# Half of the softmax sums from ScalarE in two attentions, a later time-bias step, and four destination columns in the last expert layer of a decoder

## The chip, the cores and the metric

The kernel runs on one core of a Trainium2 chip. The metric is the device time of one launch, in microseconds. One execution is also recorded by the hardware profiler, and all rows in this document come from such recordings.

## The reference, cut to what matters

The reference is a decoder of four layers on `x` of 16 x 128 tokens with 256 features. Each layer is `x = x + attention(layernorm(x))`, then a second mixing step with a context `ctx`, then a feed-forward step. Three of its twelve steps are touched.

```python
# layer 3, cross attention with a time bias ("l3x"): 16 heads of 16, 4 heads of values
pairwise_delta = |cumulative time of query - cumulative time of key|
scores = scores + time_bias_weight * log1p(pairwise_delta)
scores = scores + (1 - mask) * -1e9
w = softmax(scores);  out = (w @ v) @ Wo

# layer 2, feed-forward step, first half ("l2fa"): plain self attention, 16 heads of 16
w = softmax(q @ k.T * 0.25);  out = (w @ v) @ wo

# layer 3, feed-forward step ("l3f"): 8 experts, the best 2 of them for each token
out = zeros
for e in range(8):
    h = relu(xf @ W1[e] + b1[e]);  y = h @ W2[e] + b2[e]
    out = out + gate[:, e:e+1] * y
```

## The kernel before, in words

Every step of the decoder is a block. In a block each engine (TensorE, VectorE, ScalarE, GpSimd, and SyncE for transfers) has a program of its own in fixed order, and engines meet at semaphores. A block ends at a barrier.

**`attention_block`** serves six attentions. Its loop runs over `t` from 0 to `T + VALUES + 1`; in `l2fa` and `l3x` `T` is 32: 16 sequences (`NB`) times two sets of `HEADS = 8` heads, each set in two banks of `UNIT = 4` heads. At step `t`:

- TensorE makes the scores of `t` (L658), a slice of the projections of the next pair of sequences (L599 to L617: transposed rows, keys, queries, values), the transposition of the probabilities of `t - 3` (`turn`, L676), the product with the values of `t - 4` (L690, L695), and every second step the output projection (L631). There are three score banks, so the scores of `t + 1` wait until ScalarE has finished the exponentials of the first bank of `t`.
- VectorE adds the bias (L872, `l3x` only) and takes the maxima (L874), sums the exponentials of `t - 1` over the keys (L882) and inverts the sums (L888), empties projections (L785 in `l2fa`: the keys, which in `l3x` are ScalarE's), and copies the first bank of transposed probabilities (L898).
- ScalarE computes the exponentials, one instruction for each head (L1025, four to a bank), copies the second bank of transposed probabilities (L1041), empties some projections (L988: eight pieces of the keys in `l3x`, once for every four steps) and copies the output of the values (L1049), which the output projection L631 waits for.
- GpSimd multiplies the exponentials with the inverted sums (L953).

**The opening of `l3x`.** SyncE issues loads in this order: context, the times `fside` as `deltas`, the mask as `keywide` (spread over 128 partitions, 1 MB), context. TensorE's first instruction is L587, the running sums of the times, which waits for `deltas` and `keywide`. Then come the first query projection (from rows the block before left ready), the context's transposition, keys and values; then the four `bias_turns` (L627). VectorE copies the running sums (L842), spreads `deltas` into `dwide` in four instructions (L844), takes part in the projections and the layer norm's statistics, subtracts (L824), waits for ScalarE's absolute values and logarithms (L1014, L1016), and makes all four quarters of the bias (L861) before the first scores are touched.

**`sorted_experts_block`**, as `l3f`, sorts tokens by expert into tiles of 128 rows. There are always `NT = 39` tiles, some of them without real rows. SyncE loads the rows of tile `n` (L1259), TensorE transposes them (`turn`, L1398), multiplies by the first weights (`first_layer`, L1410) and the second (`second_layer`, L1420). As this is the last block, the results go straight into `out`: GpSimd fetches the rows so far (L1852), VectorE adds the tile's gated result (L1720), and GpSimd scatters the rows back (L1856). A token has two experts, so the fetch of a tile waits until the scatter of the tile before has landed. The rows that both transfers go to are computed by VectorE in `aim(n)` (L1684 to L1699, `dest`); there were two columns of `dest`, taken in turn.

VectorE's order in that loop is:

```python
for n in range(NT):
    if n + 1 < NT:
        relu(n + 1)
        aim(n + 1)
    if n + 2 < NT:
        empty_rows(n + 2)
    empty_out(n)
```

`aim(n)` waits for the scatter of tile `n - 2`. `empty_rows(n + 2)` (L1675) lets TensorE start the first weights of tile `n + 2`; `empty_out(n)` is L1715 and L1720. SyncE loads tile `n` after tile `n - 2` was transposed and aimed (`turned`, `dest_ready`).

## Time and profile before

| what | value |
|---|---|
| time, median of 3 runs | 2975.32 us (2972.42 to 2977.95) |
| the profiled execution's own time | 2969.33 us |
| its span in the profile | 2967.4 us |
| mean granted TensorE clock, share of full speed | 0.933 |
| `l2fa`, first to last scores | 1774.5 to 1923.1 us |
| `l3x`, first load to first scores | 2312.5 to 2336.0 us |
| `l0x`, first load | 243.8 us |
| `l3x`, first to last scores | 2336.0 to 2524.9 us |
| `l3f`, first fetch to last scatter | 2649.3 to 2956.5 us |

A row of the timeline has the start in us from the span's start, the length in us, the engine, the line and operation, what it writes and reads, how many instructions are merged, and in brackets how long the engine sat idle before it and what ended that. TensorE's multiplications are PE, its weight loads PEld, VectorE is DVE, ScalarE ACT, GpSimd POOL; a q behind the name is an engine's instruction queue. The ends of the multiplications are modelled, so a busy PE is not a full one.

### The profile page before, as it was taken

What the parts mean: (1) busy time and instruction counts of PE and PEld (TensorE: products, weight loads), DVE (VectorE), ACT (ScalarE), POOL (GpSimd) and SP (SyncE); (2) the same over time, 40 slices, a digit from 0 to 9 for tenths busy, and PEclk for the clock granted to TensorE, in tenths of its full rate; (3) what the DMA queues carried; (4) which work ended last, traced back from release to release, by engine and by line L of the source; (5) the groups of instructions that cost most, each with busy time, mean ns of one, the idle gap of its engine ahead of it and who ended that gap; (6) DMA issues with size and microseconds to landing.
All of it is one profiled execution on the core that took longest, in us unless ns stands there. A gap on an engine that the chain in (4) does not pass through costs nothing. (4 is left out here: it accounts for less than half of the span.)

```text
span 2967.4 us, 47859 instructions
## 1 busy us (share of the span) xinstructions
PE 2559.4 (86%) x16117; PEld 1874.6 (63%) x16117; DVE 1810.5 (61%) x4091; ACT 1313.7 (44%) x3205; POOL 808.7 (27%) x627
## 2 busy tenths in 40 slices
PE   4998989999688785999998989959969687869997
PEld 2666756666455453777676767649945465448886
DVE  7866976589788544344455559953355688444443
ACT  2334654266778234434343436623332565323332
POOL 5533520054000332222221216621110243132222
PEclk8999999999888798999999999979989898989999
DMA  9001000000200423000001010051120300531110
GB/s 321 2 1 49 14 19 1 15 1 1 65 4 1 109 87 125 29 1 1 1 1 50 12 42 31 2 206 37 37 76 1 90 12 1 182 118 49 51 49 26
DMA packets 152050, 142.43 MB, mean 48 GB/s; under 512 B 59948, under 2 KB 136770, under 8 KB 151428
## 3 DMA queue, kind: packets, MB, share of 16 engines
q1 hardware_dynamic: 139668, 110.61, 12.6%
q0 software_dynamic: 10560, 27.19, 2.7%
q8 instruction: 135, 2.21, 0.3%
q10 hardware_dynamic: 1584, 1.57, 0.2%
q14 instruction: 103, 0.84, 0.1%
HBM read 98.14 MB, written 43.02 MB: 48 GB/s over the span
## 5 line engine op out<-in xcount | busy, mean ns | idle before, releaser
L953 POOL TENSOR_TENSOR room<-room 128x1024 f32<-128x1024 f32 x144 | 273.1, 1896 | 464.0 <-DVE room L888 463.7
L882 DVE TENSOR_REDUCE room<-room 128x8 f32<-128x1024 f32 x144 | 174.1, 1209 | 0.0
L1420 PE MATMUL l3f_out<-room,Y 128*128 x624 | 141.0, 379 | 0.0
L953 POOL TENSOR_TENSOR room<-room,Y 128x1024 f32<-128x1024 f32 x32 | 60.7, 1896 | 252.0 <-DVE Y L888 252.0
L1420 PEld LDWEIGHTS l3f_out<-room,Y 128*128 128x128 f32 x624 | 115.6, 190 | 14.2
L1025 ACT ACTIVATE room<-l2a_scores,Y 128x128 f32<-128x128 f32 x256 | 71.9, 380 | 86.7 <-DVE Y L874 86.7
L609 PE MATMUL l2a_proj<-room 128*128 128x256 f32 x384 | 97.5, 398 | 11.6 <-ACT room L977 11.6
L2461 POOL DMA_INDIRECT sorted_rows<-room,l1f_place_i x32 | 31.0, 968 | 267.1 <-DVE l1f_place_i L2172 257.7
L1025 ACT ACTIVATE room<-l3x_scores,room 128x128 f32<-128x128 f32 x256 | 73.3, 401 | 55.3 <-DVE room L874 55.3
L1025 ACT ACTIVATE room<-l1a_scores,room 128x128 f32<-128x128 f32 x256 | 71.4, 386 | 58.6 <-DVE room L874 58.6
L1025 ACT ACTIVATE room<-l0x_scores,room 128x128 f32<-128x128 f32 x256 | 70.5, 384 | 59.4 <-DVE room L874 59.4
L1025 ACT ACTIVATE room<-l2fa_scores,room 128x128 f32<-128x128 f32 x256 | 71.4, 389 | 49.2 <-DVE room L874 49.1
L609 PEld LDWEIGHTS l2a_proj<-room 128*128 128x128 f32 x384 | 71.8, 196 | 24.7 <-issue 14.9
L1420 PE MATMUL l2fm_out<-room,Y 128*128 x368 | 83.1, 379 | 0.0
L914 POOL MEMSET room<- 128x3072 f32 (+1 forms) x4 | 9.4, 2338 | 269.1 <-POOLq L135 269.1
L1811 ACT COPY l3f_yn<-room 128x2048 f32 x39 | 74.5, 1911 | 16.4 <-DMA sorted_rows<-l3f_yn,l3f_place_i 16.2
L1410 PEld LDWEIGHTS l3f_hidden<-Y,l3f_yn 128*128 128x128 f32 x640 | 74.9, 195 | 10.7 <-DVE Y L1675 10.5
L1410 PE MATMUL l3f_hidden<-Y,l3f_yn 128*128 128x128 f32 x640 | 77.9, 281 | 4.3 <-DVE Y L1675 4.1
L1410 PE MATMUL l3f_hiddenT<-Y,l3f_yn 128*128 128x128 f32 x608 | 72.6, 278 | 7.2 <-DVE Y L1675 6.9
L1410 PEld LDWEIGHTS l3f_hiddenT<-Y,l3f_yn 128*128 128x128 f32 x608 | 69.5, 192 | 13.5 <-DVE Y L1675 13.4
L1856 POOL DMA_INDIRECT out<-Y,l3f_dest x39 | 39.1, 1002 | 135.2 <-DVE Y L1720 131.8
L3517 DVE TENSOR_TENSOR room<-room 128x2048 f32<-128x2048 f32 x32 | 72.2, 2289 | 3.9 <-ACT room L3623 2.6
(838 smaller groups left out, 6909.3 us busy)
## 6 DMA issues: line engine op xcount, KB each, us to landing
sorted_rows<-head SPq DMA_DIRECT2D x1, 16640.0 KB, 57.0
room<-in_L_ffn_w SPq DMA_DIRECT2D x16, 1024.0 KB, 13.0
room<-in_L_ffn_W SPq DMA_DIRECT2D x16, 1024.0 KB, 12.0
Y<-sorted_rows SPq DMA_DIRECT2D x62, 130.0 KB, 2.1
room<-in_ctx SPq DMA_DIRECT2D x24, 256.0 KB, 2.9
room<-sorted_rows SPq DMA_DIRECT2D x39, 130.0 KB, 2.1
room<-results SPq DMA_DIRECT2D x8, 512.0 KB, 7.1
room<-in_L_ffn_routed_w SPq DMA_DIRECT2D x4, 512.0 KB
```

Of the source, the lines that this page charges most:

```text
L609: mm = pe.matmul(bank[:, (c - i) * PT:(c - i + 1) * PT], w.v[kind][:, kc, c * P:(c + 1) * P], (y_of(g) if kind == "q" else c_of(g))[:, kc, ...
L882: dve.tensor_reduce(rsum[:, u % 2, :], p[:, u % (TURN + 1), :, :], AX.X, ALU.add)
L914: pool.memset(v[:, :, :, :], 0.0).then_inc(v_zeroed, 1)
L953: pool.tensor_tensor(p[:, u % (TURN + 1), :, :], p[:, u % (TURN + 1), :, :], rinv[:, u % (TURN + 1), :].unsqueeze(2).to_broadcast([P, HEAD ...
L1025: op = act.activation(p[:, t % (TURN + 1), a * UNIT + i, :], bank[:, i * P:(i + 1) * P], ACT.Exp, bias=nmx[:, t % 2, a * UNIT + i:a * UNIT ...
L1410: mm = pe.matmul(hidden[n % 2][a][:, q * P:(q + 1) * P], stage[:, n % 2, kc * F + f * P:kc * F + (f + 1) * P], rowsT[:, n % 2, kc, :], sta ...
L1420: mm = pe.matmul(obank[n % 2][:, 0:D], hT[:, n % 2, f, :], chip.room[:, bass.ds(at + (SLOT // 2 + f * D), D)], start=(f == 0), stop=(f == ...
L1811: act.copy(stage[:, n % 2, :], chip.room[:, bass.ds(at, KC * F)]).then_inc(staged, 1)
L1856: pool.indirect_dma_start(final_rows, bass.IndirectOffsetOnAxis(dest[:, n % 2:n % 2 + 1], 0), result[:, n % 2, :], None, bounds_check=TOK ...
L2461: pool.indirect_dma_start(table[:, :], bass.IndirectOffsetOnAxis(place_i[c][:, b:b + 1], 0), yn[:, b, :], None).then_inc(scattered, 16)
L3517: dve.tensor_tensor(hat[:, n % 2, those, :], hat[:, n % 2, those, :], aw[:, g % 2, j, those].unsqueeze(2).to_broadcast([P, HALF, NR]), ALU ...
```

## The change

It has three parts.

1. In `l3x` and `l2fa` the exponentials of heads 4 to 7 write their own sums (`accum_out`), and L882 sums only heads 0 to 3.
2. In the opening of `l3x` the matmul of the running sums goes behind the opening projections, on VectorE the spreading of `deltas` goes behind the emptied projections, and only the first quarter of the bias is made ahead of the loop, the others at steps 1 to 3.
3. In the last expert block `dest` has four columns, and `aim(n)` waits for the scatter of tile `n - 4` in place of `n - 2`.

```diff
+    SUMMED = UNIT if t_ in ("l3x", "l2fa") else HEADS
...
                 w.wait(pe)
-                if plan.mask == "timebias":
-                    pe.wait_ge(raw_loaded[0], 32)
-                    pe.matmul(out[:, 0:NB], chip.upper[:, :], deltas[:, :], start=True, stop=True).then_inc(ct_ready, 1)
...
-                for f in opening + bias_turns:
+                for f in opening:
+                    project((0, f))
+                if plan.mask == "timebias":
+                    pe.wait_ge(raw_loaded[0], 32)
+                    pe.matmul(out[:, 0:NB], chip.upper[:, :], deltas[:, :], start=True, stop=True).then_inc(ct_ready, 1)
+                for f in bias_turns:
                     project((0, f))
...
-                if plan.mask == "timebias":
-                    dve.wait_ge(ct_ready, 1)
-                    dve.tensor_copy(ctcol[:, :], out[:, 0:NB])
-                    for n in range(NB // 4):
-                        dve.tensor_copy(dwide[:, n * 4:n * 4 + 4, :], ...).then_inc(wide_ready, 1)
-                    dve.drain()
...
                 for f in opening:
                     if not by_scalar(f):
                         empty((0, f))
+                if plan.mask == "timebias":
+                    dve.wait_ge(raw_loaded[0], 32)
+                    for n in range(NB // 4):
+                        dve.tensor_copy(dwide[:, n * 4:n * 4 + 4, :], ...).then_inc(wide_ready, 1)
+                    dve.wait_ge(ct_ready, 1)
+                    dve.tensor_copy(ctcol[:, :], out[:, 0:NB])
+                    dve.drain()
                 if chip.has_head:
                     statistics()
...
+                def biased(n):
+                    dve.wait_ge(log_ready, n + 1)
+                    dve.scalar_tensor_tensor(out=bias[:, n * 4:n * 4 + 4, :], ...)
+                    dve.drain()
...
-                    for n in range(NB // 4):
-                        dve.wait_ge(log_ready, n + 1)
-                        dve.scalar_tensor_tensor(out=bias[:, n * 4:n * 4 + 4, :], ...)
-                    dve.drain()
+                    biased(0)
...
-                        dve.tensor_reduce(rsum[:, u % 2, :], p[:, u % (TURN + 1), :, :], AX.X, ALU.add)
+                        dve.tensor_reduce(rsum[:, u % 2, 0:SUMMED], p[:, u % (TURN + 1), 0:SUMMED, :], AX.X, ALU.add)
...
+                    if plan.mask == "timebias" and 1 <= t < NB // 4:
+                        biased(t)
...
-                        op = act.activation(p[:, t % (TURN + 1), a * UNIT + i, :], bank[:, i * P:(i + 1) * P], ACT.Exp, bias=nmx[...])
+                        h = a * UNIT + i
+                        if h < SUMMED:
+                            op = act.activation(p[:, t % (TURN + 1), h, :], bank[:, i * P:(i + 1) * P], ACT.Exp, bias=nmx[...])
+                        else:
+                            op = act.activation(p[:, t % (TURN + 1), h, :], bank[:, i * P:(i + 1) * P], ACT.Exp, bias=nmx[...],
+                                                accum_out=rsum[:, t % 2, h:h + 1])
...
+    DESTS = 4 if last else 2
...
-                    if n >= 2:
+                    if last and n >= 4:
+                        dve.wait_ge(returned[par], (n // 2 - 1) * 16)
+                    if not last and n >= 2:
                         dve.wait_ge(returned[par], n // 2 * 16)
...
-                    dve.scalar_tensor_tensor(out=dest[:, par:par + 1], ...).then_inc(dest_ready, 1)
+                    dve.scalar_tensor_tensor(out=dest[:, n % DESTS:n % DESTS + 1], ...).then_inc(dest_ready, 1)
```

The fetch and the scatter of GpSimd take their column with `n % DESTS` too.

## Rows read from the trace of the kernel before

**Rows 1.** Stretches: length, busy time (instructions) by engine, granted clock, DMA share, GB/s.

```profile
255.00:413.00 158.00, 153.60 (x1272) 107.68 (x1273) 139.12 (x267) 99.23 (x332) 77.88 (x50) 0.99 0.05 13
...
1774.50:1923.10 148.60, 136.59 (x1184) 103.31 (x1183) 136.91 (x266) 97.36 (x332) 94.42 (x66) 0.97 0.09 29
...
2336.00:2525.00 189.00, 149.66 (x1212) 111.25 (x1211) 156.95 (x288) 122.47 (x386) 67.03 (x40) 0.89 0.04 12
...
2660.00:2930.00 270.00, 258.88 (x1742) 234.81 (x1741) 113.03 (x448) 100.48 (x172) 69.72 (x69) 1.00 0.16 49
```

**Rows 2.** Timeline of the opening of l3x.

```profile
2319.74 0.58 PE L587 MATMUL l3x_out<-room,upper 128*128 128x16 f32 x2 [9.41 <-DMA room<-in_mask_BxS_ff]
...
2320.15 3.47 PE L609 MATMUL l3x_proj<-head,room 128*128 128x256 f32 x8
...
2330.04 4.55 PE L627 MATMUL l3x_proj<-upper,room 128*128 128x128 f32 x24 [2.28 <-ACT room L988]
...
2337.60 2.81 DVE L861 SCALAR_TENSOR_TENSOR room<-room,vecs 128x512 f32<-128x512 f32 x4 [0.21 <-issue]
...
2342.01 1.14 ACT L1025 ACTIVATE room<-l3x_scores,room 128x128 f32<-128x128 f32 x4 [1.07 <-DVE room L874]
```

**Rows 3.** Timeline of the opening of l0x, a block with the same order of projections.

```profile
246.58 0.82 PEld L604 LDWEIGHTS l0x_proj<-ident,room 128*128 128x128 f32 x4 [0.35 <-DMA room<-in_ctx]
```

**Rows 4.** Groups of VectorE's and ScalarE's instructions in l2fa: busy time, mean ns | idle before.

```profile
L874 DVE TENSOR_REDUCE room<-l2fa_scores 128x4 f32<-128x512 f32 x64 | 40.7, 678 | 4.7 <-PE l2fa_scores L658 4.6
L882 DVE TENSOR_REDUCE room<-room 128x8 f32<-128x1024 f32 x32 | 38.7, 1209 | 0.0
...
L1025 ACT ACTIVATE room<-l2fa_scores,room 128x128 f32<-128x128 f32 x256 | 71.4, 389 | 49.2 <-DVE room L874 49.1
```

**Rows 5.** Waits of TensorE in l2fa, 1776 to 1923 us: total, times, longest.

```profile
PE l2fa_probsT L676 <- DVE room L898: 5.4, 8, 0.8
```

**Rows 6.** Timeline of ScalarE in an earlier block that sums while it activates.

```profile
1171.03 0.19 ACT L2441 ACTIVATION_READ_ACCUMULATOR room<-X 128x1 f32 x1
1171.12 0.40 ACT L2441 ACTIVATE room<-X 128x256 f32<-128x256 f32 x1
```

**Rows 7.** Timeline of l3x around the emptied keys, two groups of four steps.

```profile
2396.19 1.10 PE L631 MATMUL l3x_proj<-room 128*128 128x256 f32 x4 [1.71 <-ACT room L1049]
...
2467.30 3.06 ACT L988 ACTIVATE room<-l3x_proj,block_of 128x256 f32<-128x256 f32 x8
...
2470.67 2.05 PE L631 MATMUL l3x_proj<-room 128*128 128x256 f32 x4 [1.71 <-ACT room L1049]
...
2472.51 3.62 PE L609 MATMUL l3x_proj<-room 128*128 128x256 f32 x8
```

**Rows 8.** Timeline of l3f, from one fetch to the next.

```profile
2791.93 0.16 DVE L1684 TENSOR_TENSOR vecs<-Y,vecs 128x1 f32<-128x1 f32 x1 [1.79 <-DMA out<-Y,l3f_dest]
...
2792.82 1.03 POOL L1852 DMA_INDIRECT Y<-out,l3f_dest  x1 [2.34 <-DMA out<-Y,l3f_dest]
...
2793.89 15.31 SPq L1259 DMA_DIRECT2D Y<-sorted_rows  x3
...
2795.57 0.48 DVE L1720 SCALAR_TENSOR_TENSOR Y<-Y,vecs 128x256 f32<-128x256 f32 x1 [1.44 <-DMA Y<-out,l3f_dest]
...
2796.39 1.13 DVE L1707 TENSOR_SCALAR Y<-l3f_hiddenT,vecs 128x128 f32<-128x128 f32 x4 [0.34 <-issue]
...
2800.10 1.03 POOL L1852 DMA_INDIRECT Y<-out,l3f_dest  x1 [2.25 <-DMA out<-Y,l3f_dest]
```

**Rows 9.** The chain that ended last, in order of time: two fetches of tiles without real rows.

```profile
2932.52 3.13 DMA Y<-out,l3f_dest
...
2940.01 2.15 DMA Y<-out,l3f_dest
```

**Rows 10.** DMA issues in l3f: count, median us from issue to landing.

```profile
Y<-out,l3f_dest POOLq DMA_INDIRECT x39, 2.9
out<-Y,l3f_dest POOLq DMA_INDIRECT x39, 2.5
```

More of the change, by code:

```diff
@@ L856, in _ @@
                     empty((0, f))
+                def biased(n):
+                    dve.wait_ge(log_ready, n + 1)
+                    dve.scalar_tensor_tensor(out=bias[:, n * 4:n * 4 + 4, :], in0=gap[:, n * 4:n * 4 + 4, :], scalar=w.v["tb"],
+                                             in1=keywide[:, n * TG:(n + 1) * TG].rearrange("p (j k) -> p j k", j=4), op0=ALU.mult, op1=ALU.add)
+                    dve.drain()
                 if plan.mask == "timebias":
                     dve.wait_ge(key_ready, 1)
-                    for n in range(NB // 4):
-                        dve.wait_ge(log_ready, n + 1)
-                        dve.scalar_tensor_tensor(out=bias[:, n * 4:n * 4 + 4, :], in0=gap[:, n * 4:n * 4 + 4, :], scalar=w.v["tb"],
-                                                 in1=keywide[:, n * TG:(n + 1) * TG].rearrange("p (j k) -> p j k", j=4), op0=ALU.mult, op1=ALU.add)
-                    dve.drain()
+                    biased(0)
                 for t in range(T + VALUES + 2):
@@ L1024, in exps @@
                     for i in range(UNIT):
-                        op = act.activation(p[:, t % (TURN + 1), a * UNIT + i, :], bank[:, i * P:(i + 1) * P], ACT.Exp, bias=nmx[:, t % 2, a * UNIT + i:a * UNIT + i + 1])
+                        h = a * UNIT + i
+                        if h < SUMMED:
+                            op = act.activation(p[:, t % (TURN + 1), h, :], bank[:, i * P:(i + 1) * P], ACT.Exp, bias=nmx[:, t % 2, h:h + 1])
+                        else:
+                            op = act.activation(p[:, t % (TURN + 1), h, :], bank[:, i * P:(i + 1) * P], ACT.Exp, bias=nmx[:, t % 2, h:h + 1],
+                                                accum_out=rsum[:, t % 2, h:h + 1])
                     op.then_inc(exps_done, 1)
@@ L1191, in sorted_experts_block @@
         row_at = chip.iota_i[:, 0:NT]
-        dest_f, dest = own("dest_f", [P, 2, 2]), own("dest", [P, 2], mybir.dt.uint32)
+        dest_f, dest = own("dest_f", [P, 2, 2]), own("dest", [P, DESTS], mybir.dt.uint32)
         hT = flat_y[:, 0:2 * F].rearrange("p (a f t) -> p a f t", a=2, f=HC)
@@ L1698, in aim @@
                     dve.drain()
-                    dve.scalar_tensor_tensor(out=dest[:, par:par + 1], in0=dest_f[:, par, 1:2], scalar=real[:, n:n + 1], in1=dump[:, n:n + 1], op0=ALU.mult, op1=ALU.add).then_inc(dest_ready, 1)
+                    dve.scalar_tensor_tensor(out=dest[:, n % DESTS:n % DESTS + 1], in0=dest_f[:, par, 1:2], scalar=real[:, n:n + 1], in1=dump[:, n:n + 1], op0=ALU.mult, op1=ALU.add).then_inc(dest_ready, 1)
                 def relu(n):
@@ L1851, in _ @@
                             pool.wait_ge(returned[(n - 1) % 2], ((n - 1) // 2 + 1) * 16)
-                        pool.indirect_dma_start(so_far, None, final_rows, bass.IndirectOffsetOnAxis(dest[:, n % 2:n % 2 + 1], 0),
+                        pool.indirect_dma_start(so_far, None, final_rows, bass.IndirectOffsetOnAxis(dest[:, n % DESTS:n % DESTS + 1], 0),
                                                 bounds_check=TOK - 1, oob_is_err=False).then_inc(fetched, 16)
@@ L1855, in _ @@
                     if last:
-                        pool.indirect_dma_start(final_rows, bass.IndirectOffsetOnAxis(dest[:, n % 2:n % 2 + 1], 0), result[:, n % 2, :], None,
+                        pool.indirect_dma_start(final_rows, bass.IndirectOffsetOnAxis(dest[:, n % DESTS:n % DESTS + 1], 0), result[:, n % 2, :], None,
                                                 bounds_check=TOK - 1, oob_is_err=False).then_inc(returned[n % 2], 16)
```

2 lines of the change are left out of this document (1 added, 1 removed).

## The prediction, made before the changed kernel ran

> **What bounds the kernel now.** I read the page first for the shares of the engines, then the stretches of the three touched blocks, then in each block the waits, the timeline and, for the last one, the chain that ended last. The blocks have different limits, so each edit is priced in its own.
>
> In the loop of `l2fa` TensorE is busy 136.6 of 148.6 us and VectorE 136.9 [rows 1]. The reader is to see that TensorE is nearly full: it idles 12.0 us, and in `l0x`, a loop of the same form, 4.4 of 158. So at most some 8 us are to be had there, however much VectorE is relieved. Its waits name VectorE's copy L898 with 5.4 us in 8 waits [rows 5].
>
> In the loop of `l3x` TensorE is busy 149.7 of 189 us at a granted clock of 0.89, VectorE 157.0 [rows 1]. Here no engine is full; the timeline shows a cycle of four steps. VectorE runs without a pause through two or three steps; then ScalarE empties the keys in 3.06 us, so its copy L1049 comes late, and TensorE waits 1.71 us with the output projection L631 [rows 7]. In the later group that L631 takes 2.05 us where the earlier one took 1.10: the clock fell from 2.4 to 1.2 GHz after TensorE had idled, and the projection behind it takes 3.62 us [rows 7].
>
> In the opening of `l3x` TensorE stands until 2319.74 for the mask's broadcast, 7.3 us after the block's first load at 2312.5 (table above) and after 9.41 us of standing idle [rows 2], though the query projection behind it needs no load of this block.
>
> In `l3f` GpSimd waits for VectorE's L1720 or for a landed scatter, and L1720 waits for the fetch [rows 8]: fetch, add, scatter, fetch is one serial chain. From 2660 to 2930 us TensorE ran 1742 matmuls at full clock [rows 1], 50 to a tile (32, 16 and 2 transposes), so 34.8 tiles: 7.75 us for a tile, of which TensorE is busy 7.43. The chain sets the pace, and TensorE is close behind.
>
> **The opening of `l3x`.** The query projection now starts with the block, about 2312.5 in place of 2320.15: 7.65 us earlier [rows 2]. It takes 3.47 us, to 2316.0. In `l0x` the context was there 2.8 us after its load (load at 243.8 in the table, transposition at 246.58 when it had landed [rows 3]), so here by 2315.3, no wait. Context, keys and values keep their distances and end near 2320, just behind the broadcast at 2319.7. The moved matmul L587 costs TensorE 0.58 us [rows 2] between the values and L627, where TensorE waited 2.28 us for the emptied keys [rows 2]; that wait covers it. Without that cover it would cost its 0.58. VectorE's spreading of the times is covered by the same wait. So L627 and all that follows on it comes 7.65 us earlier.
>
> The bias: four quarters took 2.81 us, 0.70 each [rows 2]. Now one stands before the first scores. ScalarE waited 1.07 us for VectorE at its first exponentials [rows 2], and only that much is gained, because behind it stand ScalarE's own logarithms and table load. The three other quarters go into steps 1 to 3: 2.1 us more on VectorE, against 3 x 0.53 us that it is relieved of (below), so 0.5 net; another 0.4 for ScalarE's longer steps there. Sum: -7.65 - 1.07 + 0.9 = -7.8; I take -8, bounds -5 (context late or broadcast still in the way) and -9.
>
> **The sums.** L882 takes 1209 ns for 1024 elements in a partition; L874, a reduction of 512, takes 678 [rows 4]. The halved L882 saves 0.53 us a step, 32 times in each block. ScalarE's price: before, four exponentials stood in 1.14 us [rows 2]; one lasts 0.39 [rows 4], so they follow each other by (1.14 - 0.39) / 3 = 0.25. With a sum a read of 0.19 us is added, and the next instruction starts 0.09 us after the read did, so a pair lasts as long as the activation itself (0.40 for 256 elements) [rows 6]. Here that is 0.39 in place of 0.25: 0.14 x 4, or 0.5 us a step (0.56 rounded down, as the mean of 0.39 holds stalled ones). No row shows an exponential of 128 elements with a sum; the bounds are 4 x 0.09 = 0.4 and 4 x 0.19 = 0.8 us.
>
> A rule beside it: the Trainium skill (ScalarE: Activation LUTs, What ACT_TABLE_LOAD costs) gives 280 ns + 0.833 ns for each element with a pointer as bias, and 93 ns of overlap between neighbours. By it an exponential takes 387 ns and follows by 294, so the sum would add only 0.09 to each, 0.37 us a step; the trace's 0.25 disagrees, and I go by the trace.
>
> *In `l2fa`* ScalarE is busy 97 of 149 us [rows 1], which hides 0.5 us a step. VectorE's L898 comes 0.53 us earlier in each of the 8 waits of 0.68 us: 8 x 0.53 = 4.3 us, and with a second halved sum in the same group a little more. -5.5, bounds 0 (TensorE takes no advantage) and -8 (the idle share of `l0x`).
>
> *In `l3x`* the cycle of four steps goes: two steps on VectorE (-0.53 each), then ScalarE's second four exponentials (+0.5), copy, keys, L1049, then TensorE to the next scores. Net -0.56, seven times: -4. What is queued behind the longer exponentials is L1041, L988 and L1049, and TensorE waits for the last. TensorE's own idle time ahead of L631 grows by 0.5 us, as it arrives 1.06 us earlier and is released 0.56 earlier. The clock fell in 4 of 6 groups although the wait was 1.71 us in both rows [rows 7], so the fall is not decided by that wait alone, and more idle time makes it likelier. At half clock L631 and L609 take 2.05 + 3.62 = 5.7 us, at full about half plus latencies, 3.0 (1.10 for L631): 2.7 us a fall. One more fall, taken at +2 for its chance. -2, bounds -14 (no fall any more: -4 and 4 x 2.7 back) and +5 (three more falls).
>
> **Four destination columns.** `aim(n + 1)` waited for a landed scatter, which ended at 2791.93 [rows 8]. But the fetch waits for that same landing, and VectorE then waits 1.44 us for the fetch anyway [rows 8]. TensorE gains `empty_rows` earlier, but L1720 waits for the fetch and not for TensorE. So the wait that goes is covered by the chain of transfers, and its removal alone is worth nothing. What is moved is the load of rows by SyncE, which follows `aim`. Before, it was issued at 2793.89, 1.07 us behind the fetch and 1.96 us behind the landing [rows 8]. After, `aim` follows `relu` at once: 2796.39 + 1.13 + 1.96 = 2799.5, which is 0.6 us ahead of the fetch at 2800.10 [rows 8]. Both fetches of [rows 9] carry no rows: 3.13 us beside a load, 2.15 without one. A full fetch takes 2.9 us where a full scatter, which has no load beside it, takes 2.5 [rows 10]. So the load costs a fetch about 0.4 us now. Ahead of the fetch its data may be through sooner: I take 0.1 us off, 34 full tiles: -3. Bounds: -0.32 x 34 = -11, where TensorE's 7.43 us a tile sets the pace, and +0.98 x 34 = +33, the full price of [rows 9] on top of today's.
>
> A rule speaks against this part: the Trainium skill (DMA: Bandwidth & Descriptors, Queues, rings and completion order) says a transfer's completion is written only after every earlier write of the same DMA engine, across queues. The page would make a load moved ahead delay each fetch's completion; the 3.13 against 2.15 us of the empty fetches agrees that a completion can wait for a load's data. By it the sum would end near the slow rival below.
>
> **The sum.** -8 - 5.5 - 2 - 3 = -18.5 us. It is made in the profiled execution, whose own time is 2969.33 us (span 2967.4 and 1.9 around it): 2950.8 there. The median of the runs is 6.0 us above that execution, so the forecast is 2975.3 - 18.5 = 2956.8 us. For this kernel 0.2%, 6 us, is about what a measurement can tell from no change.
>
> **The rivals.**
>
> *The last block speeds up to TensorE's pace.* The load leaves the fetch's way altogether. For it: 0.4 us a fetch to win. Against: load and fetch still start within 0.6 us of each other. -8 - 5.5 - 2 - 11 = -26.5: 2949 us.
>
> *The sums change nothing, only the opening gains.* In `l2fa` TensorE is full, in `l3x` ScalarE's 0.5 us or the clock eats VectorE's 0.53. For it: TensorE's 92% in `l2fa` [rows 1]. Against: the 5.4 us that TensorE waits for L898 [rows 5]. With the last block unchanged: -8, 2967 us. Should the broadcast still hold the opening (its bound, -5), the whole change is within what can be measured.
>
> *Slower: the row load stands in front of the fetch.* Place: the fetch L1852 in 34 tiles of `l3f`. Price: up to 0.98 us each. It eats the other 15.5 us of gain from 0.46 us a tile on and makes the kernel slower by over 0.2% from 0.63 on; at 0.98 it gives 2975.3 - 15.5 + 33 = 2993 us. For it: [rows 9]. Against: the load now starts earlier, and most of its data may be through before the fetch has its descriptors, whose making takes 1.03 us [rows 8].
>
> **How the numbers follow.** Forecast 0.55, with a range of its own of 2950 to 2963; last block at TensorE's pace 0.15; opening alone 0.18; load in front 0.12. The first two are faster, of the third 0.13; of the load's cases 0.05 end within 0.2% and 0.07 above. Faster 0.83, same 0.10, slower 0.07. The range, 2943 to 2972, takes in the first three with their bounds and leaves out the last.
>
> **What would show each step.** The first exponentials of `l3x` start about 21 us behind the block's first load, not 29.5. L882 on 512 elements near 0.68 us; reads of 0.19 us behind half of the exponentials, and four with sums in about 1.6 us. TensorE's wait for L898 in `l2fa` near 1 us. In `l3x` L631 still waiting for L1049, and longer than 1.71 us. In `l3f` no wait ahead of L1684, loads issued ahead of the fetches, and the fetch's median to landing against 2.9 us, which decides the last block. The prediction fails if that median rises by half a microsecond, or if TensorE's clock in `l3x` moves far from 0.89.

## The result, and the profile after

The changed kernel takes 2948.0 us (median of 4 runs, 2941.3 to 2950.5) where the kernel before takes 2973.9 (median of 4, 2972.4 to 2978.0). The medians lie 25.9 us apart; the ratio estimated from these runs is 0.989, with a 95% interval of 0.987 to 0.991, and a second comparison below gives 0.9888. So 26 to 33 us were gained where 18.5 were forecast. The time lies 2 us below the forecast's own range of 2950 to 2963 us and inside the wide one. The direction holds and each of the three parts gains, but the sizes are off, the last block's most.

The profiled execution has a span of 2946.8 us, 20.6 below the one before. The blocks ahead of `l2fa`, which the change doesn't touch, take up to 19 us more or less from one execution to another (`l2fa` opens at 1764.2 us before, at 1772.3 after, and between 1770 and 1784 in the other kernels below). So I compare blocks, not whole spans.

Three stretches, one in each touched block: length, busy time by engine, granted clock, DMA share, GB/s. They answer to [rows 1].

```profile
1783.00:1930.00 147.00, 138.72 (x1212) 104.49 (x1210) 125.37 (x273) 110.87 (x469) 96.41 (x67) 0.97 0.08 30
2337.00:2515.00 178.00, 147.29 (x1199) 109.02 (x1199) 136.62 (x277) 127.90 (x500) 66.52 (x40) 0.90 0.06 21
2650.00:2910.00 260.00, 258.83 (x1754) 237.37 (x1753) 110.09 (x452) 103.35 (x176) 70.22 (x69) 1.00 0.17 51
```

In `l3f` TensorE is busy 258.8 of 260 us where it was 258.9 of 270 [rows 1]: the block has closed up. That TensorE is nearly always busy doesn't mean that it sets the pace. VectorE's add (L1737), which the scatter waits for, still stands idle until the fetch lands, 111.8 us in all:

```profile
L1737 DVE SCALAR_TENSOR_TENSOR Y<-Y,vecs 128x256 f32<-128x256 f32 x39 | 18.9, 484 | 111.9 <-DMA Y<-out,l3f_dest 111.8
```

In `l3x` the granted clock is still 0.90, so it didn't move from the 0.89 before.

The opening of `l3x` in the timeline, in answer to [rows 2].

```profile
2316.55 0.37 SPq L567 DMA_DIRECT2D room<-in_ctx  x1
...
2316.59 2.93 PE L607 MATMUL l3x_proj<-head,room 128*128 128x256 f32 x8 [2.20 <-PEq L135]
...
2323.99 0.40 PE L636 MATMUL l3x_out<-room,upper 128*128 128x16 f32 x2
...
2326.39 5.53 PE L625 MATMUL l3x_proj<-upper,room 128*128 128x128 f32 x32 [2.00 <-ACT room L997]
...
2333.49 0.75 DVE L864 SCALAR_TENSOR_TENSOR room<-room,vecs 128x512 f32<-128x512 f32 x1 [0.21 <-issue]
...
2335.08 1.28 ACT L1026 ACT_TABLE_LOAD   x1
2336.37 1.14 ACT L1036 ACTIVATE room<-l3x_scores,room 128x128 f32<-128x128 f32 x4
```

The query projection starts with the block's first load. The first exponentials come 19.8 us behind that load, and ScalarE's table load (L1026), no longer VectorE, stands right ahead of them. Before it was 29.5 us (2342.01 in [rows 2], less 2312.48). The clock has a part in this, beside the moved matmul. In the ten profiles with the old opening the distance is 29.4 to 29.9 us where the granted clock averages 0.74 over it (four profiles, this one among them) and 31.5 to 31.9 us where it averages 0.66 or 0.67 (the other six). With the new opening it is 19.8 to 20.8 us at 0.83 (six profiles). The granted clock is at half from 2312.9 to 2323.2 us in the profile before, most of it while TensorE stands idle; for 17.1 us in the second profile of that kernel; and for 3.4 us (2317.4 to 2320.8) in the changed one.

ScalarE in the same block, one step: four plain exponentials, then four that sum.

```profile
2340.87 1.14 ACT L1036 ACTIVATE room<-l3x_scores,room 128x128 f32<-128x128 f32 x4 [1.46 <-DVE room L881]
2342.24 0.37 ACT L1038 ACTIVATE room<-l3x_scores,room 128x128 f32<-128x128 f32 x1 [0.23 <-DVE room L881]
2342.51 0.19 ACT L1038 ACTIVATION_READ_ACCUMULATOR room<-l3x_scores,room 128x1 f32 x1
2342.60 0.36 ACT L1038 ACTIVATE room<-l3x_scores,room 128x128 f32<-128x128 f32 x1
2342.85 0.20 ACT L1038 ACTIVATION_READ_ACCUMULATOR room<-l3x_scores,room 128x1 f32 x1
2342.94 0.36 ACT L1038 ACTIVATE room<-l3x_scores,room 128x128 f32<-128x128 f32 x1
```

With a sum an exponential follows its neighbour by 0.34 us (2342.94 - 2342.60); plain ones by 0.25 ((1.14 - 0.37) / 3, rounded down as before). So a sum costs 0.09 us, not the 0.14 of the prediction. (Medians over the loop: 343 and 250 ns.)

Waits of TensorE in `l2fa` (first row) and in `l3x` (the others): total, times, longest. They answer to [rows 5] and [rows 7].

```profile
PE l2fa_probsT L679 <- DVE room L905: 1.2, 1, 1.2
...
PE l3x_proj L629 <- ACT room L1063: 14.7, 6, 2.5
PE l3x_probsT L679 <- DVE room L905: 6.6, 14, 1.0
PE l3x_scores L661 <- ACT room L1036: 6.6, 9, 2.5
```

The `l2fa` wait is down from 5.4 us. In `l3x` the output projection waits 2.5 us in five of six times and 2.1 in the first, where it waited 1.71, and what stands behind the wait in the timeline runs slow, for a part of its time at 1.2 GHz in place of 2.4:

```profile
2440.91 2.04 PE L629 MATMUL l3x_proj<-room 128*128 128x256 f32 x4 [2.52 <-ACT room L1063]
2442.75 2.38 PE L607 MATMUL l3x_proj<-room 128*128 128x256 f32 x8
```

Behind all six of these waits L629 or L607 ran slow (before: behind 4 of 6). In five L629 itself took 1.48 to 2.04 us in place of 1.10, in the sixth L607 took 3.46.

The last block, `l3f`, from one scatter to the next fetch, in answer to [rows 8].

```profile
2768.32 0.15 DVE L1701 TENSOR_TENSOR vecs<-Y,vecs 128x1 f32<-128x1 f32 x1
...
2769.34 0.42 DVE L1690 COPY Y<-l3f_logits_ps 128x256 f32<-128x256 f32 x1
...
2769.81 3.84 PE L1425 MATMUL l3f_hidden<-Y,l3f_yn 128*128 128x128 f32 x32
...
2770.24 15.36 SPq L1274 DMA_DIRECT2D Y<-sorted_rows  x3
2771.11 1.03 POOL L1869 DMA_INDIRECT Y<-out,l3f_dest  x1 [2.37 <-DMA out<-Y,l3f_dest]
```

The row of the load has three loads merged in it; its start is what counts here. `aim` (L1701) waits for nothing, the load is issued 0.87 us ahead of the fetch, and TensorE starts the tile's matmuls 1.30 us ahead of it. The DMA view gives a fetch a median of 2.8 us (2.9 in [rows 10]) and a scatter 2.4.

### The profile page after: what moved, and what is told of

The parts are those of the page before. It is cut to its first block and busy times, and to the rows that moved or that the text cites. A ratio compares the mean times of both kernels' runs of the same rounds, so it can differ in the third digit from the quotient of the medians.

```text
span 2946.8 us, 48117 instructions
## 1 busy us (share of the span) xinstructions
PE 2569.8 (87%) x16117; PEld 1884.3 (64%) x16117; DVE 1775.6 (60%) x4091; ACT 1339.4 (45%) x3461; POOL 809.3 (27%) x627
## 3 DMA queue, kind: packets, MB, share of 16 engines
q8 instruction: 135, 2.21, 0.3%
q10 hardware_dynamic: 1584, 1.57, 0.2%
## 5 line engine op out<-in xcount | busy, mean ns | idle before, releaser
L889 DVE TENSOR_REDUCE room<-room 128x8 f32<-128x1024 f32 (+1 forms) x144 | 139.9, 971 | 0.7 <-ACT room L1038 0.6
L607 PE MATMUL l2a_proj<-room 128*128 128x256 f32 x384 | 97.5, 398 | 11.6 <-ACT room L986 11.6
L607 PEld LDWEIGHTS l2a_proj<-room 128*128 128x128 f32 x384 | 71.8, 196 | 24.7 <-issue 14.9
L1737 DVE SCALAR_TENSOR_TENSOR Y<-Y,vecs 128x256 f32<-128x256 f32 x39 | 18.9, 484 | 111.9 <-DMA Y<-out,l3f_dest 111.8
L1435 PEld LDWEIGHTS l2fm_out<-room,Y 128*128 128x128 f32 x368 | 68.2, 190 | 8.4
L881 DVE TENSOR_REDUCE Y<-l2a_scores 128x4 f32<-128x512 f32 x64 | 41.2, 686 | 52.7 <-PE l2a_scores L668 52.7
```

The source lines that it names most:

```text
L607: mm = pe.matmul(bank[:, (c - i) * PT:(c - i + 1) * PT], w.v[kind][:, kc, c * P:(c + 1) * P], (y_of(g) if kind == "q" else c_of(g))[:, kc, ...
L881: op = dve.tensor_reduce(nmx[:, t % 2, a * UNIT:(a + 1) * UNIT], bank, AX.X, ALU.max, negate=True)
L889: dve.tensor_reduce(rsum[:, u % 2, 0:SUMMED], p[:, u % (TURN + 1), 0:SUMMED, :], AX.X, ALU.add)
L1435: mm = pe.matmul(obank[n % 2][:, 0:D], hT[:, n % 2, f, :], chip.room[:, bass.ds(at + (SLOT // 2 + f * D), D)], start=(f == 0), stop=(f == ...
L1737: op = dve.scalar_tensor_tensor(out=result[:, n % 2, :], in0=result[:, n % 2, :], scalar=gate[:, n % 2, 0:1], in1=so_far, op0=ALU.mult, op ...
```

## The experiments

All times are compared as ratios to the kernel before on the same chip, with their 95% intervals. The lengths of blocks are from one profile of each kernel. "Block" of `l3x` is from the end of TensorE's work in the block ahead to the end of its own (before 232.7 us, after 219.4; 229 to 236 in the eight further profiles of an unchanged one); of `l2fa`, TensorE's first to last instruction (before 176.0, after 169.2); of `l3f`, the first scatter to the last (before 293.4, after 282.0).

**Which part gives what.** Each of the three parts of the diff alone, and the whole change once more.

> Part 1 alone: half of the sums from ScalarE in l2fa and l3x; opening and last block as before. Theory A (each part acts in its own block and the parts add): l2fa gains about 5 us and the loop of l3x about 3.5, 8 to 9 us in all, a ratio near 0.997; the last block's loop, first scatter to last, stays at 293 us as before. Rival B (the three parts share one gain, for instance because the clock of TensorE follows the whole history): the last block changes too, or the two attentions gain clearly less than 8 us.

> Part 2 alone: the running sums behind the projections, one quarter of the bias ahead of the loop. Theory A: the first exponentials of l3x come 19.8 us behind the block's first load in place of 29.5; 2 us come back in the first steps where VectorE now makes three quarters of the bias; net about 9 us, ratio near 0.997. Rival B: the gain is given back in the loop of l3x, because without the halved sums VectorE has no room for the three quarters: net 5 us or less.

> Part 3 alone: four destination columns in the last block. Theory A (the moved row load no longer delays the fetch): first scatter to last 282 us in place of 293, ratio near 0.996, fetches with a median of 2.78 us and none above 3.0. Rival B (the profile of the kernel before had unlucky transfers in its last block, and the gain is noise): about 290 us and a ratio near 0.999.

> The changed kernel once more, beside its three parts on one chip. Theory A: the three parts add, 9 + 9 + 11 = 29 us, a ratio near 0.990. Rival: the true change is nearer to the forecast of 18.5 us, a ratio of 0.994, and the first measurement was favoured by its runs.

| kernel | ratio (95%) | `l2fa` | `l3x` | `l3f` |
|---|---|---|---|---|
| sums alone | 0.9953 (0.9936 to 0.9970) | 168.6 | 227.3 | 296.4 |
| opening alone | 0.9966 (0.9948 to 0.9983) | 176.5 | 219.3 | 298.9 |
| four columns alone | 0.9951 (0.9932 to 0.9971) | 176.0 | 232.4 | 282.4 |
| the whole change | 0.9888 (0.9870 to 0.9906) | 169.5 | 219.2 | 282.2 |

The sums give 7 us in `l2fa`. In `l3x` they give 5.4 alone and nothing beside the new opening. The four columns give 11 us against the profile before, and more against the unchanged last blocks of the two other kernels. Each part acts in its own block, as theory A had it each time. Two sizes were missed: the sums gave 14 us of the kernel's time (0.0047) where 8 to 9 were expected, and with four columns alone two fetches, of 4.28 and 3.58 us, stand above the expected 3.0.

**Is it the row load?** To the kernel with four columns alone I added a hold on the load: it waits for the scatter, by way of six small operations on VectorE that nobody uses (the texts below call them seven or eight).

```diff
+                    if last and n >= 3:
+                        sp.wait_ge(load_free, n - 2)
                     sp.dma_start(rows[:, n % 2, :], table[bass.ds(at, P), :]).then_inc(rows_in[n % 2], 16)
...
+                    if last and n + 3 < NT:
+                        free_load(n)     # wait for the scatter, six small operations, then_inc(load_free)
```

Three more kernels: `aim(n + 1)` put ahead of `relu(n + 1)`; the load cut to 16 rows of one number from the third tile on (the tiles repeat old rows, so most of the output is left out); and the kernel before once more.

> The four columns alone, but the row load is held back to its old place: VectorE makes its columns early and frees the next rows' transposition at once, then waits for the landed scatter, runs seven small operations of the same sizes on scratch columns, and only then lets the load go. Theory A (the gain of the last block is the moved load and what it no longer meets): first scatter to last goes back to 293 to 299 us, fetches of full tiles to a median of 2.85, and several transfers of over 3.2 us come back. Rival B (the gain is that TensorE and VectorE are no longer held by the landing): it stays near 282 us.

> The four columns alone, with VectorE making the columns ahead of the relu: the row load goes out 1.1 us earlier still, about 2 us ahead of the fetch. Theory A (load in the fetch's way): the fetches fall to 2.5 us like the scatters, and first scatter to last from 282 to some 272 us, unless TensorE's 7.3 us a tile binds first. Rival B: the load now meets the scatter, scatters grow from 2.44 by what the fetches lose, and the stretch stays at 282.

> The four columns alone, and from tile 2 on the row load brings one number into each of 16 partitions (the tiles then repeat old rows, so most of the output is left out). It prices the load in the fetch's way. Theory A: full fetches fall from 2.80 to about 2.5 us; first scatter to last about 275. Rival: the fetch is slower than the scatter by itself, stays near 2.8, and the load costs it nothing.

> The kernel before, recorded once more. Its last block from first scatter to last was 293, 296 and 299 us in three recordings of kernels that leave it as it was. Theory A: 293 to 299 again, with transfers of over 3.2 us only where a packet of code is loaded beside them. Rival: a value near 285 would make part of the gain chance.

The late load took the gain back: 0.9984 (0.9968 to 1.0000), block 296.7 us. I read that as the load's place being the whole cause. The other three spoke against so simple a view. With `aim` first the load starts earlier still, 2.35 us ahead of the fetch, and the block is longer (286.8; ratio 0.9957, 0.9944 to 0.9971), not the 272 of theory A; fetches and scatters kept medians of 2.80 and 2.47, so rival B, with longer scatters, doesn't fit either. With next to no load the block is 283.4, no better than the changed kernel, and the fetch keeps its 2.8 us: the rival there held, and an early load costs the fetch nothing. The kernel before gave 301.2 in its second profile, so the unchanged block itself varies by 8 us.

**Where the block's time is.** Take, in each profile, the time from issue to landing of every fetch and scatter between the first scatter and the last (76 transfers), and add it up. It is 208.6 us in the kernel before and 197.2 in the changed one. What is left of the block is 84.8 us in both, and 84.7 or 84.8 in all sixteen profiles but one (85.3 with TensorE late, below). So the block differs by the lengths of its transfers and by nothing else, and in none of these kernels does TensorE set its pace. What is to be explained is why the transfers are longer in some kernels.

A transfer that was long gave the next idea. This is the DMA view of one fetch of the kernel before, issued at 2734.93 us and landed 4.81 us later. The row of GB/s has 40 slices; a queue's row has its packets, MB, and share of 16 engines. The fetch is on q0 (32 packets of data, and 16 of 4 bytes that tell of completion), the row load on q1 (128 rows and 16 of 4 bytes). The sizes come from the packets' own records in the trace.

```profile
GB/s 0 0 0 0 0 0 0 0 0 0 0 0 0 0 201 234 234 218 270 238 331 220 236 26 17 0 0 0 0 0 9 8 8 8 8 8 17 0 0 0
...
q0 software_dynamic: 48, 0.13, 10.3%
q1 hardware_dynamic: 144, 0.13, 8.6%
q8 instruction: 1, 0.02, 1.3%
```

And a fetch of the changed kernel (2778.50, landed after 2.62).

```profile
GB/s 0 0 0 0 69 83 153 55 139 236 305 305 264 139 28 0 0 0 0 0 0 0 0 0 0 109 329 164 246 164 55 55 0 0 0 0 0 0 0 0
...
q1 hardware_dynamic: 144, 0.13, 18.0%
q0 software_dynamic: 48, 0.08, 8.7%
```

The first has a packet of the kind "instruction" beside it, a load of program code of 16 KB: 1.3% of 16 engines for 4.9 us, so 1.0 us on one DMA engine. Most of the data has moved by the 25th slice; then nothing for five slices, then a trickle of 8 GB/s. Three narrower windows of the same fetch say what was held up: 2734.9 to 2737.7, 2737.7 to 2737.98 and 2738.66 to 2739.8 us. Between the last two no packet starts.

```profile
q0 software_dynamic: 47, 0.13, 17.9%
q1 hardware_dynamic: 128, 0.12, 12.5%
...
q8 instruction: 1, 0.02, 22.2%
q1 hardware_dynamic: 7, 0.01, 5.6%
...
q1 hardware_dynamic: 9, 0.01, 4.8%
q0 software_dynamic: 1, 0.00, 0.1%
```

The fetch has 47 of its 48 packets done before the code load starts, 2.77 us behind the issue. The 48th, one of its sixteen completions, starts 3.75 us behind it, as the code load ends (2.77 + 1.00), and so do the last eight rows of the row load, a sixteenth of 128. The trace doesn't name a packet's engine, but this fits one of the sixteen DMA engines being held by the code load.

In the sixteen profiles 79 fetches and scatters of this block took over 3.2 us. All of them had a packet of a code load (queue q8 or q14) beside them, and in all of them fifteen of the sixteen completions were there 2.8 us behind the issue and the sixteenth came later. Of the fetches of the first 35 tiles, 28 had a packet of q8 that started 0.6 to 2.2 us behind their issue: their mean is 4.08 us, and 27 took over 3.2. The 497 with no code load starting in that stretch have a mean of 2.83, and 7 took over 3.2. (For scatters: 78 with a mean of 3.17, and 408 with 2.46.) With no code load beside it at all a fetch took 2.8 us (2.9 beside a row load) and a scatter 2.44, in all kernels. The number of code loads is the same in both kernels, 17 on q8 and 18 on q14. What differs is where they fall.

Whose code is it? The packets of q8 come at the same places of TensorE's program in all sixteen profiles, to within 20 matmuls (counted from the first fetch, the fifth packet comes behind 466 to 472 matmuls, the last behind 1816 to 1822), also in the three kernels below that give VectorE eight steps more for each tile. In those three q14 has 21 packets in place of 18, and q8 its 17. Over the whole changed kernel q8 brings 2.21 MB, and of the instructions that its profile counts TensorE ran 32,234, VectorE 4,091 and ScalarE 3,461. So q8 goes with TensorE's program and q14 with VectorE's.

**TensorE's start or the load's place?** If the code loads of q8 move with TensorE's program, its start against the fetch decides what they meet. Three kernels to tell that from the load's place: the kernel before with the small load; four columns and an early load, but VectorE held by the scatter behind `empty_rows` ("VectorE late" in the table); and the same with the hold ahead of `empty_rows`, so that TensorE's matmuls wait too ("TensorE late").

> The kernel before, with its two destination columns and every wait of them, but with the row loads of the last block cut to 16 rows of one number each from the third tile on (the tiles repeat old rows, so most of the result is left out). Theory: the four columns pay only because the big load no longer lies beside the fetch. Then the waits can stay and the load can go: the last block from its first scatter to its last is 282 to 285 us, as in the changed kernel (282.0) and in the one with four columns and the small load (283.4), and the kernel's time is 0.995 of the one before, as with the four columns alone. Rival: the wait of the destinations itself costs (VectorE and TensorE start each tile late): the block stays at 290 us or more, of the 293.4 to 301.2 that the kernel before shows.

> The four destination columns alone, the row load as early and as large as they make it, but VectorE made to wait for the scatter in the next tile's work as it did before (the wait and eight small operations on numbers that nobody uses), so that TensorE's matmuls of the next tile start as late against the transfers as before. It is the kernel with the late load without the hold on the load. Theory from the small loads: the load is worth 1 to 4 us, and where TensorE's 16 KB code loads fall against the transfers is worth the rest; with VectorE held they fall into the landing of fetches and scatters again (4 to 6 of 16 of them, 1 in the changed kernel), and the block is 290 to 297 us. Rival, that the load's place is the whole gain: the load is early here, so the block is 282 to 285 us as with the four columns alone.

```diff
-                    if last and n >= 3:
-                        sp.wait_ge(load_free, n - 2)
```

> The kernel with VectorE's work held and the load left early, with two statements turned: VectorE's wait for the scatter now stands before it empties the next tile's transposed rows (L1678), not behind. So TensorE's first matmuls of a tile wait for the scatter again, as in the kernel before, while the row load stays ahead of the fetch and the four columns stay. Theory: what pays is TensorE's lead over the fetch. Those matmuls start 1.2 to 1.3 us ahead of the fetch in the fast last blocks (282 to 285 us) and 0.62 us behind it in the slow ones (293 to 301). Here they start behind the fetch, TensorE's 16 KB code loads fall into the transfers again (10 or more of 16 of them begin 0.7 to 2.9 us behind an issue, long transfers over 3.2 us are 5 or more), and the block is 291 to 297 us. Rival, that the load's place is the gain: it is early here, so the block stays at 282 to 287 us.

```diff
+                    if last and n + 3 < NT:
+                        free_load(n)
                     if n + 2 < NT:
                         empty_rows(n + 2)
-                    if last and n + 3 < NT:
-                        free_load(n)
```

In the table, "start" is the median of TensorE's first matmul of a tile against the fetch's issue; "met" counts those of the 17 code loads of q8 that start at least 0.6 us behind the issue of a fetch or scatter and 0.3 before its landing; "transfers" is the sum over the 76 transfers.

| kernel | start us | row load | met | transfers | `l3f` | ratio (95%) |
|---|---|---|---|---|---|---|
| before | +0.62 | beside the fetch | 13 | 208.6 | 293.4 | 1 |
| before, again | +0.62 | beside the fetch | 14 | 216.4 | 301.2 | one execution |
| before, small load | +0.62 | next to none | 13 | 208.3 | 293.1 | 0.9987 (0.9974 to 1.0001) |
| TensorE late | +0.62 | ahead | 12 | 206.1 | 291.3 | 0.9989 (0.9977 to 1.0001) |
| late load | -0.36 | beside the fetch | 9 | 212.0 | 296.7 | 0.9984 (0.9968 to 1.0000) |
| `aim` first | -1.00 | beside the scatter | 7 | 202.1 | 286.8 | 0.9957 (0.9944 to 0.9971) |
| VectorE late | -1.28 | ahead | 2 | 200.1 | 284.9 | 0.9957 (0.9939 to 0.9974) |
| four columns, small load | -1.27 | next to none | 4 | 198.6 | 283.4 | one execution |
| four columns | -1.22 | ahead | 3 | 197.7 | 282.4 | 0.9951 (0.9932 to 0.9971) |
| after | -1.26 | ahead | 2 | 197.2 | 282.0 | (whole change) |

The timeline of the kernel with TensorE late shows the cut: load 0.84 us ahead of the fetch, the matmuls 0.62 behind it.

```profile
2791.28 7.77 SPq L1262 DMA_DIRECT2D Y<-sorted_rows  x2
...
2792.12 1.03 POOL L1873 DMA_INDIRECT Y<-out,l3f_dest  x1 [2.35 <-DMA out<-Y,l3f_dest]
...
2792.27 0.42 DVE L1678 COPY Y<-l3f_logits_ps 128x256 f32<-128x256 f32 x1
2792.74 3.65 PEld L1413 LDWEIGHTS l3f_hidden<-Y,l3f_yn 128*128 128x128 f32 x32 [0.43 <-DVE Y L1678]
```

The kernel before with the small load stayed slow, as its rival said: to take the load away and leave the waits gains nothing clear of noise. The kernel with VectorE late gave the number of its rival, 284.9 us (the theory had 290 to 297). Taken alone that spoke for the load's place; but TensorE starts early there too, since VectorE is held only behind `empty_rows`. The third kernel decides: with TensorE late and the load still early the block is 291.3 us, 12 of 17 code loads meet a transfer, 7 transfers took 3.3 us or more, and most of the gain is gone, as its theory said. VectorE may wait, if TensorE does not. In the kernel with the late load TensorE waited for the rows themselves (10 times, 10.9 us), and 9 code loads met a transfer. So TensorE's start carries most of the gain, some 7 to 10 us; the load's place is worth the 0.1 us a fetch between 2.9 and 2.8, some 3 us. No run took the code loads away or moved them alone, so the link from TensorE's start to the code loads to the long transfers rests on where the packets fall in sixteen profiles, not on a kernel without them.

**The clock in `l3x`.** Theory: the sums make ScalarE's copy L1063 later, TensorE waits longer, its clock falls in every group, and that eats their gain. I tried the copy ahead of the emptied keys, the sums in `l2fa` alone, and both.

> The changed kernel, with one order turned in the attention with the time bias: ScalarE copies the values' output (L1063) first and empties its share of the keys and queries behind it. Theory: the matmuls of L629 wait at the head of a turn for that copy, and TensorE's clock is below 2.4 GHz in the group that follows (7 of 7 groups in the changed kernel, where L629 takes 1.3 to 2.05 us instead of 1.10). With the copy first the wait is shorter by the emptying (about 0.8 us), the lowered clock is gone in most groups, the loop goes from 183.5 to 176 to 180 us and the block from 219.4 to 212 to 216; the kernel is 0.1 to 0.25% faster than the changed one. Rival: the emptied keys are then what is late, the head of the next projection waits for them in place of the copy, and the block stays within 1 us of 219.4 or gets 1 to 4 us longer.

```diff
-                    for x in at[(t, 1)]:
-                        if by_scalar(x[1]):
-                            empty(x)
                     ...                          # the copy L1063 of the values' output
+                    for x in at[(t, 1)]:         # in the block with the time bias alone
+                        if by_scalar(x[1]):
+                            empty(x)
```

> The changed kernel with ScalarE's sums in the first attention only; the one with the time bias has its sums from VectorE again. Theory: with the new opening the sums buy nothing there, since they make the matmuls of L629 wait longer for ScalarE and so lower TensorE's clock in every group: the block is 219 us, as with the opening alone (219.2), clock falls in 1 or 2 groups of 7, the first attention stays at 169.2, and the kernel's time is within 0.1% of the changed one's. Rival: the 5.4 us that the sums alone gave in that block are still in the changed kernel, and the block goes to 223 to 225.

```diff
-    SUMMED = UNIT if t_ in ("l3x", "l2fa") else HEADS
+    SUMMED = UNIT if t_ in ("l2fa",) else HEADS
```

> Both edits of the two kernels before it: ScalarE copies the values' output first, and takes sums in the first attention only. Theory: the wait of L629 for the copy is shortest here (ScalarE has neither the sums nor the emptying in front of the copy), the clock stays at 2.4 GHz in the loop, and the block goes to 212 to 217. Rival, the loop is held by VectorE's sums of eight heads once TensorE's wait is gone: the block stays at 219 while the same order with ScalarE's sums is shorter.

| kernel | ratio (95%) | `l3x` | its loop, mean clock | wait ahead of L629 |
|---|---|---|---|---|
| after | 0.9888 (0.9870 to 0.9906) | 219.4 | 0.90 | 14.7 us, 6 |
| sums in `l2fa` alone | 0.9907 (0.9891 to 0.9922) | 221.8 | 0.92 | 9.0 us, 6 |
| copy first | 0.9850 (0.9834 to 0.9867) | 204.4 | 0.96 | none |
| copy first, sums in `l2fa` alone | 0.9876 (0.9860 to 0.9891) | 209.0 | 0.96 | none |

The changed kernel has six such waits, not the seven of the first text. The copy first is worth 15 us in the block, where I had put 3 to 7 on it, and the kernel beats the changed one by about 0.4% (0.9850 / 0.9888; the intervals don't meet). Its loop as a stretch (the granted clock is the third number from the end), its longest wait, and one turn of the timeline:

```profile
2341.00:2507.00 166.00, 139.22 (x1224) 103.44 (x1224) 139.44 (x283) 128.78 (x508) 67.88 (x40) 0.96 0.07 21
```

```profile
PE l3x_proj L607 <- ACT room L997: 8.2, 6, 1.6
```

```profile
2435.63 1.03 PE L629 MATMUL l3x_proj<-room 128*128 128x256 f32 x4
2438.23 1.99 PE L607 MATMUL l3x_proj<-room 128*128 128x256 f32 x8 [1.57 <-ACT room L997]
```

The same two groups of matmuls, summed over the loop of the kernel after (first two rows) and of the one with the copy first: busy, mean ns | idle before.

```profile
L607 PE MATMUL l3x_proj<-room 128*128 128x256 f32 x104 | 32.4, 467 | 0.0
...
L629 PE MATMUL l3x_proj<-room 128*128 128x256 f32 x52 | 17.8, 475 | 14.7 <-ACT room L1063 14.7
```

```profile
L607 PE MATMUL l3x_proj<-room 128*128 128x256 f32 x104 | 27.9, 416 | 8.2 <-ACT room L997 8.2
...
L629 PE MATMUL l3x_proj<-room 128*128 128x256 f32 x52 | 13.4, 380 | 0.0
```

Two things were gained: 6.5 us of waiting (14.7 - 8.2) and 8.9 us less for the same matmuls, which had run in part at 1.2 GHz (50.2 - 41.3); together 15.4, the block's 15. The wait did move to the keys, as the rival had it, but it is 0.95 us shorter each time (2.52 less 1.57) and the clock stays at 2.4 GHz behind it, without a break from 2368 to 2508 us. Which of the two took the slow groups away, the shorter wait or its place behind L629, no run here tells apart. 

The sums buy 4.6 us once the copy is first (209.0 - 204.4), and 0 to 2.4 while it isn't. The theory for the sums in `l2fa` alone held only in part: waits back at 1.71 us, slow groups behind two of six, a clock of 0.92, but 2.4 us more in the block, with VectorE again summing eight heads. (A slow group is one whose L629 or L607 ran slow.) With the opening alone, which has the same loop, that block took 219.3, and the 2.5 us between them go with one slow group more (two against one).

The same holds for the old loop in its nine profiles with the sums on VectorE: from the first exponentials to the last it took 184.0 us with three slow groups, 184.9 to 187.3 with four and 188.2 to 188.3 with five. So one profile of this block can't settle 2 us. With both edits the block is 209.0, below the 212 to 217 expected, and the rival (219) is refuted.

## Why the prediction was right or wrong

**Opening: right, a little short.** Forecast -8, measured -9.7 at the first exponentials with the whole change, and -13.4 over the block with the opening alone. L636 was hidden by TensorE's wait for the emptied keys as said (2.00 us remain of it). Of the 13.4 with the opening alone, 8.7 are there at the first exponentials (20.8 against 29.5 us) and the rest came in the loop: one slow group of six, four before. I had priced neither that nor the clock in the opening itself, where the query projection took 3.47 us before and 2.93 after.

**Sums in `l2fa`: right.** Forecast -5.5, measured -7 (169.2 to 169.5 against 176.0), the wait for L905 down from 5.4 to 1.2 us as forecast. L889 on 512 elements takes 0.67 us as worked out. (Two slips of arithmetic change nothing: 8 x 0.53 is 4.2, not 4.3, and the bounds in `l3x` come to -14.8 and +4.1, not -14 and +5.)

**ScalarE's price of a sum: mis-sized.** Forecast 0.14 us each, measured 0.09. My error was to carry the pair of [rows 6] over from 256 elements to 128: there a pair lasts as long as the activation (0.40 us), here 0.34 where the activation takes 0.36, and I had put the mean of 0.39 in its place. The Trainium skill (ScalarE: Activation LUTs, What ACT_TABLE_LOAD costs) had given 0.09, as an estimate from its overlap of 93 ns; the trace disagrees with the page on the spacing itself (0.25, not 0.29), but not on the increment.

**Sums in `l3x`: right in kind.** "More idle time makes it likelier": the clock now falls in every group. Forecast -2 on top of the opening, measured 0 (219.3 with the opening alone, 219.2 to 219.4 with both). The parts alone make 14.0, 10.2 and 14.6 us of a kernel of 2987.6, together 38.8; joined they make 33.5. The 5 us between agree with this block's 5.4, but each part's interval is 5 us wide to either side, so the whole times alone don't show it; the blocks do.

**Four columns: the step that failed.** Forecast -3, measured -11 in the block and -15 in the kernel's time. The words were: "TensorE gains `empty_rows` earlier, but L1720 waits for the fetch and not for TensorE. So the wait that goes is covered by the chain of transfers, and its removal alone is worth nothing." The chain was read rightly: it is the transfers and 84.8 us around them, before and after. What failed is the last step: that L1720 doesn't wait for TensorE was true, but that the removed wait is then worth nothing took the transfers' lengths as given. They fell by 11.4 us in all (208.6 to 197.2), as TensorE's start went from 0.62 us behind the fetch to 1.26 ahead and the code loads that meet a transfer from 13 to 2 of 17. Only the 0.1 us a fetch for the load was as forecast. The signs were there in the trace, unread: a fetch of 4.81 us in a chain whose median is 2.9.

**The rivals.** "TensorE's pace" gave 2949 us, and the time came to 2948, but that is in part luck. Its cause (the load leaves the fetch's way altogether) is not the one measured, TensorE doesn't set the pace although it is busy 258.8 of 260 us, and the gain in `l3x` and `l2fa` was larger than in its sum. "Only the opening gains" is refuted by 168.6 us in `l2fa`. The slow rival is refuted by the fetch's median, 2.8 us with the load 0.87 ahead of it. The rule on completions (the Trainium skill, DMA: Bandwidth & Descriptors, Queues, rings and completion order), which spoke for it, fits the code loads instead: the trace agrees where the last completion of the 4.81 us fetch starts as the code load ends, and one packet of 1.0 us put off a fetch's landing by up to 2 us.

## What to carry to other kernels

A serial chain of transfers can be shortened by an engine that isn't in it: add up the transfers and see what is left, look at their spread and not at the median alone, and at what runs beside the long ones. Where an engine waits for the last of several things that another one makes in a row, ask whether it can be made first; behind a shorter wait TensorE kept its clock here, and that was worth more than the wait itself (8.9 us against 6.5). Parts that are priced one by one overlap where they relieve the same cycle: here 5 us in `l3x`.

## What the hardware showed that was not expected

Where a code load of one packet (16 KB, 1.0 us on one of 16 DMA engines) started 0.6 to 2.2 us behind the issue of a fetch, the fetch took 4.08 us in the mean in place of 2.83; a fetch took as much as 4.8 us, a scatter as much as 4.6 in place of 2.44. Around a transfer's issue it cost less: fetches kept medians of 2.77 to 2.85, scatters had medians of 2.38 to 2.88. The clock of TensorE stayed at 2.4 GHz behind waits of 1.57 us between busy stretches, was lower behind 1 to 5 of the six waits of up to 1.71, depending on the kernel, and behind nearly all of 2.1 and 2.5 us (five of six with the sums alone, all six in the whole change).
